# Attention 0 of a fused two-layer decoder: block 0 for all head groups first, then blocks 1 to 3 group by group, with the inputs of blocks 1 to 3 turned by DMA inside the first slots

## The reference, cut to what matters

```
q = (layernorm(x) @ wq).reshape(32, 64, 32, 128)
k = repeat((ctx @ wk).reshape(32, 64, 8, 128), 4)
v = repeat((ctx @ wv).reshape(32, 64, 8, 128), 4)
scores = einsum('bqhd,bkhd->bhqk', q / sqrt(128), k)
out = einsum('bhqk,bkhd->bqhd', softmax(scores), v)
x = x + out.reshape(32, 64, 4096) @ wo
x = x + ffn0(layernorm(x))        # fp8-like quantised weights W0, W1
x = x + attention1(layernorm(x), ctx)
x = x + ffn1(layernorm(x))
```

## Time and profile before

| | |
|---|---|
| median of 3 runs | 1656.03 us (1653.91 to 1657.03) |
| the profiled execution's own time | 1652.99 us |
| its span | 1651.3 us |
| PE busy, share of the span | 1499.1 us, 91% |
| DVE | 1237.5 us, 75% |
| ACT | 825.6 us, 50% |
| POOL | 267.0 us, 16% |
| first projection of attention 0 | at 56.95 us |
| scores of the first slot | at 74.68 us |
| last output product of attention 0 ends | at 1020.5 us |

### The profile page before, as it was taken

One profiled execution on the slowest core, in us unless ns is written; L12 is line 12 of the kernel. 1 busy time (PEld: TensorE's weight loads), 2 busy tenths in 40 slices (PEclk: granted clock), 3 DMA queues, 4 the chain that ended last, 5 costly groups with the idle time before them and its releaser, 6 DMA issues. The chain is left out here.

```text
span 1651.3 us, 29775 instructions
## 1 busy us (share of the span) xinstructions
PE 1499.1 (91%) x11322; PEld 796.1 (48%) x11323; DVE 1237.5 (75%) x2276; ACT 825.6 (50%) x1752; POOL 267.0 (16%) x247
## 2 busy tenths in 40 slices
PE   5799999999999999999999987799999988777695
PEld 4455455555555555555555553344444444344253
DVE  6567667668667667667767787799888885999777
ACT  3343433424324334243342332777888864888652
POOL 2001102002001011011011000001111103889620
PEclk7799999999999999999999998899999999999898
DMA  7032231321312313222221122122222350867502
GB/s 267 1 78 52 62 93 27 78 77 30 95 57 52 91 43 73 65 54 63 66 63 52 26 103 100 40 45 46 45 44 54 67 99 1 149 105 119 77 1 102
DMA packets 274121, 114.06 MB, mean 69 GB/s; under 512 B 239184, under 2 KB 255696, under 8 KB 273744
## 3 DMA queue, kind: packets, MB, share of 16 engines
q1 hardware_dynamic: 235104, 79.26, 22.2%
q10 hardware_dynamic: 38896, 33.03, 6.5%
HBM read 45.15 MB, written 11.53 MB: 34 GB/s over the span
## 5 line engine op out<-in xcount | busy, mean ns | idle before, releaser
L576 PE MATMUL pj<-XT,WQ 128*128 128x512 f16 x1536 | 338.9, 381 | 6.5 <-PEq L370 6.5
L618 PE MATMUL xp<-WO,OT 128*128 128x512 f16 x1536 | 340.5, 381 | 2.7 <-DVE X L815 2.7
L618 PEld LDWEIGHTS xp<-WO,OT 128*128 128x128 f16 x1536 | 148.3, 98 | 185.9 <-issue 14.9
L576 PEld LDWEIGHTS pj<-XT,WQ 128*128 128x128 f16 x1536 | 148.7, 98 | 182.1 <-DVE WKV L285 6.8
L696 ACT ACTIVATE E<-E 128x512 f32<-128x512 f32 x64 | 40.3, 629 | 328.1 <-DVE E L792 328.1
L815 DVE SCALAR_TENSOR_TENSOR X<-xp,X 128x512 f32<-128x512 f32 x128 | 88.4, 691 | 118.1 <-PE xp L618 117.1
L1019 PE MATMUL db<-W0T,XD 128*128 128x448 f16 x768 | 156.1, 362 | 16.5 <-DVE XD L1217 11.0
L556 POOL TENSOR_TENSOR VW<-VW,XB 128x1024 f32<-128x1024 f32 x14 | 33.0, 2357 | 770.4 <-DVE VW L98 770.4
L1037 PE MATMUL eb<-W1T,DT 128*128 128x512 f16 x672 | 147.7, 379 | 4.3 <-DMA DT<-HL 2.1
L757 DVE SCALAR_TENSOR_TENSOR QT<-pj,QT 128x512 f16<-128x512 f32 x128 | 88.1, 688 | 69.7 <-ACT QT L679 69.7
L1019 PEld LDWEIGHTS db<-W0T,XD 128*128 128x128 f16 x768 | 75.6, 100 | 94.8 <-DVE XD L1217 12.0
(11 more groups left out here) (228 smaller groups left out, 2388.7 us busy)
## 6 DMA issues: line engine op xcount, KB each, us to landing
W0T<-in_L_xattn_wq ACTq DMA_DIRECT2D x7, 1024.0 KB, 5.3
W0T<-in_L_xattn_wo ACTq DMA_DIRECT2D x7, 1024.0 KB, 5.1
CS<-in_ctx SPq DMA_DIRECT2D x4, 1024.0 KB, 10.0
X<-in_x SPq DMA_DIRECT2D x4, 1024.0 KB, 11.2
out<-X SPq DMA_DIRECT2D x8, 512.0 KB, 3.6
XB<-in_L_ffn_W ACTq DMA_DIRECT2D x28, 128.0 KB, 2.8
w0t<-XB ACTq DMA_DIRECT2D x7, 512.0 KB, 3.3
w1t<-W0T ACTq DMA_DIRECT2D x7, 512.0 KB, 3.8
```

The source lines that it names most:

```text
L576: last = pe.matmul(bank[:, :], w, src[:, b, k, tokens], start=n == 0, stop=n == 3 * KC - 1)
L618: last = pe.matmul(xp[i % 2][:, :], OT[:, a, j, i * P:(i + 1) * P], WO[:, b, j, :], start=n == 0, stop=n == 3 * REP - 1)
```

## The change

**Order.** Slots run in a new order: first block 0 of all 8 groups (`FIRST`, written out), then for each group its blocks 1 to 3 (`later`; groups 1 to 6 as a loop). The weights of each group are so loaded and split twice, 16 sets in place of 8. V has 3 buffers in place of 2.

**Start.** The separate start program is gone. Only block 0 is transposed by PE ahead of the first projection; x is loaded ahead of ctx. The projections of the first slot carry, on ACT and DVE, the split of the second group's WQ and WKV and the statistics of block 1.

**Inputs of blocks 1 to 3.** In each of the first six slots two x tiles and two ctx tiles are prepared: POOL normalises x, ACT writes the high parts (`high_inputs`, four copies of 128x512), POOL the low parts, and SP turns them by 8 DMA transposes of 128x512 f16 (`turn_inputs`) to XT and CT. DVE has the statistics of blocks 2 and 3 in slots 1 and 3.

**Moved pieces.** In the first slots ACT issues the load of WQ, WK, WV right behind the WO copy. In later slots WO's split is in t = 1, the first weight piece in t = 2 and 3, the second in t = 3 and t = 1 of the next group, the store in that t = 1. W0T is loaded at the end of the last group's t = 2.

The diff, cut to its core:

```diff
+        FIRST = [Slot(g, g, 0, g % 2) for g in range(GROUPS)]
+        def later(g, t):
+            return Slot(g * MORE + (GROUPS - 1 + t), g + GROUPS, t, t - 1)
 # SP
-            for g in range(GROUPS):
-                for t in range(SPG):
+            load_x(0)
+            sp.dma_start(C0, ctx[0:BLOCK, :].rearrange("(t p) d -> p t d", p=P)).then_inc(S["c_ld"], 16)
+            load_qkv(sp, 0)
+            sp.wait_ge(S["x_ld"], 16)
+            load_x(1)
+            sp.wait_ge(S["c_ld"], 16)
+            load_ctx(0)
+            sp.wait_ge(S["qkv_lo"], 2)
+            load_qkv(sp, 1)
+            load_o(sp, 0)
+            for b in (2, 3):
+                sp.wait_ge(S["x_ld"], 16 * b)
+                load_x(b)
+            def turn_inputs(s):
+                a, b = tiles_ahead(s)
+                for kind, (source, to) in enumerate(((XH, XT), (CH, CT))):
+                    sp.wait_ge(S["in_lo"], 2 * BT + 4 * s + 2 * kind + 2)
+                    for i in range(a, b):
+                        for part in range(2):
+                            sp.dma_start_transpose(to[:, part, :, i * P:(i + 1) * P], source[:, part, i - a, :]).then_inc(S["turned"], 16)
+                if s + 1 < AHEAD_SLOTS:
+                    load_ctx(s + 1)
+            for cur in FIRST:
+                turn_probabilities(cur)
+                if cur.n < AHEAD_SLOTS:
+                    turn_inputs(cur.n)
 # ACT
+            def first_slot(cur, nxt):
+                ahead = cur.n < AHEAD_SLOTS
+                probabilities(cur, nxt)
+                high_o(cur)
+                if cur.n < LAST:
+                    act.wait_ge(S["qkv_lo"], 2 * cur.n + 4)
+                    load_qkv(act, (cur.n + 2) % GROUPS)
+                high(nxt, (2,))
+                if ahead:
+                    high_inputs(cur.n, 0)
+                high(nxt, (3,))
+                if ahead:
+                    high_inputs(cur.n, 1)
+                high(nxt, (4,))
+                high_out(cur, 0)
+                high(nxt, (5,))
+                high_out(cur, 1)
+                if cur.n < LAST:
+                    high_q(act, cur.n + 2)
+                    high_kv(act, cur.n + 2)
+                act.wait_ge(S["o_lo"], cur.w + 1)
+                load_o(act, (cur.w + 1) % GROUPS)
+                if cur.n in (1, 3):
+                    ln_stats_scalar(act, 0, (2 + cur.n // 2,))
-            high(0, 0, range(6))
+            high_q(act, 0)
+            high_kv(act, 0)
+            high(FIRST[0], range(4))
+            high_q(act, 1)
+            ln_stats_scalar(act, 0, (1,))
+            high(FIRST[0], (4, 5))
+            high_kv(act, 1)
 # DVE
-                low(0, 0, u)
+            for u in range(4):
+                low(FIRST[0], u)
+            low_q(dve, 1)
+            dve.wait_ge(S["x_ld"], 32)
+            ln_moments(dve, 0, 1)
+            low(FIRST[0], 4)
+            ln_scales(dve, 0, 1)
+            low(FIRST[0], 5)
+            low_kv(dve, 1)
 # POOL
+            for s in range(AHEAD_SLOTS):
+                a, b = tiles_ahead(s)
+                pool.wait_ge(stats_ready, a // BT + 1)
+                if s:
+                    pool.wait_ge(S["in_lo"], 2 * BT + 4 * s - 2)
+                for i in range(a, b):
+                    normal(i)
+                for n, (full, split) in enumerate(((XN, XH), (XN, XH), (CS, CH), (CS, CH))):
+                    pool.wait_ge(S["in_hi"], 2 * BT + 4 * s + n + 1)
+                    pool.tensor_tensor(split[:, 1, n % 2, :], full[:, n % 2, :], split[:, 0, n % 2, :], ALU.subtract).then_inc(S["in_lo"], 1)
```

More of the change, by code:

```diff
@@ new lines, in _, with group @@
+            for cur in FIRST:
+                turn_probabilities(cur)
+                if cur.n < AHEAD_SLOTS:
+                    turn_inputs(cur.n)
+            def group(g, first, last):
+                for t in range(1, BLOCKS):
+                    turn_probabilities(later(g, t))
+                    if t == 1 and not first:
+                        turn_weights(g - 1, 1)
+                    if t == 3 and not last:
+                        turn_weights(g, 0)
+            group(0, True, False)
@@ L535, in load_weights @@
+            for g in range(1, LAST):
+                group(g, False, False)
+            group(LAST, False, True)
         def load_weights(queue, g):
@@ L641, in _, with slot, turned_before @@
-            pe.sem_inc(S["xp_done"], 1)
-            project(0, 0, range(6))
-            with pe.Fori(0, GROUPS - 1) as g:
-                group(g, False)
-            group(GROUPS - 1, True)
+            def slot(cur, nxt, turned=0):
+                scores(cur)
+                project(nxt, range(4), turned)
+                project(nxt, (4,))
+                weigh_values(cur, 0)
+                project(nxt, (5,))
+                weigh_values(cur, 1)
+            def turned_before(t):
+                return 16 * 8 * 2 * t
@@ new lines, in _ @@
+            pe.wait_ge(S["in_lo"], 2 * BT)
+            project(FIRST[0], range(6))
+            for cur in FIRST:
+                more = cur.n < LAST
+                slot(cur, FIRST[cur.n + 1] if more else later(0, 1), 0 if more else turned_before(1))
+                project_out(cur)
+            for t in range(1, BLOCKS):
+                cur = later(0, t)
+                slot(cur, later(0, t + 1) if t < MORE else later(1, 1), turned_before(t + 1) if t < MORE else 0)
+                project_out(cur)
@@ new lines, in _ @@
+            with pe.Fori(1, LAST) as g:
+                for t in range(1, BLOCKS):
+                    slot(later(g, t), later(g, t + 1) if t < MORE else later(g + 1, 1))
+                    project_out(later(g, t))
+            a, b, c = (later(LAST, t) for t in range(1, BLOCKS))
+            slot(a, b)
+            project_out(a)
+            slot(b, c)
+            scores(c)
+            project_out(b)
+            weigh_values(c, 0)
+            weigh_values(c, 1)
+            project_out(c)
@@ L907, in _, with probabilities @@
-            for u in range(6):
-                low(0, 0, u)
-            with dve.Fori(0, GROUPS - 1) as g:
-                group(g, False)
-            group(GROUPS - 1, True)
+            def probabilities(cur, nxt):
+                scores_less_max(cur, 0)
+                scores_less_max(cur, 1)
+                for jp in range(2):
+                    sums(cur, jp)
+                    low(nxt, jp)
+                    normalise(cur, jp)
+                low_probs(cur, 0)
+                low_probs(cur, 1)
+                low(nxt, 2)
```

626 lines of the change are left out of this document (318 added, 308 removed).

## The result

The changed kernel took 1686.37 us (median of 4 runs, 1685.48 to 1694.48), the kernel before 1654.97 us on the same chip (4 runs, 1651.53 to 1657.03). The ratio is 1.0205, 95% interval [1.0177, 1.0233]: slower by about 2%, where the forecast was 1644. The profiled execution has a span of 1683.7 us, 32.4 longer than the 1651.3 of before, at a mean granted clock of 0.963 (0.967 before).

A forecast was written before the change was run, and what follows sets the result against it. Attention 0 was taken to run at PE's own pace, its start bound by a POOL, PE, ACT, DVE chain. Terms -33.7 + 6.7 + 3.6 + 2.4 + 2.8 + 6.7 + 0.5 gave -11.0 us: forecast 1644, range 1632 to 1657.

The forecast's parts named there:

- part 5: Weight load beside PT in 7 first slots: 0.4 us of wait each, +2.8 us (0 to 25).
- rival C: PT's transposes get through only once the load's data is out: slower, 1666 to 1670; chance 0.09.
- part 3: Twice as many head group weight passes: a 0.51 us wait per added WO copy, 7 times, +3.6 us.
- Rival B: The load's and PT's queues share the engines evenly: PT lands 2.4 us later in 7 slots, 1649; chance 0.15.
- Part 1: The start: only block 0 is prepared ahead, so PE's first projection starts at 23.2 us, -33.7 us.
- Part 2: The seam to slot 0: scores wait 4.1 us for KT, then the next projection for WKV, +6.7 us (3 to 9).
- Part 4: Input splits in the first six slots cost nothing; LayerNorm statistics in slots 1 and 3 cost 1.2 each, +2.4 us.
- Part 6: Last group's t = 1 slot: extra DVE pieces make PE wait for QT and OT, +6.7 us (3 to 8).
- +0.5 for W0T: W0T's later load ends as the last PT transposes begin, and PE waits for these: +0.5 us (0 to 2).
- Rival D: The start doesn't shrink as told, or the seam costs double: 1652 to 1658, no change; chance 0.08.
- A: Small waits overlap or lie in slack, so parts 3, 4 and 5 are zero: about 1635; chance 0.20.

The follow-up runs named there:

- e4: The kernel before, with only the t = 0 slots' load of wq, wk, wv moved behind the WO copy, beside PT: 1707.04 us (1653.51 unmoved).
- e9: The changed kernel with wq loaded by four DMAs of 512-byte rows in place of one of 2 KB rows, still beside PT: 1680.34 us.
- e6: e1 with ACT's WO copy moved behind its third QT copy in the 16 slots that have one: 1632.67 us, ratio 0.9882.
- e1: The changed kernel with the load of wq, wk, wv issued at the head of each first slot, ahead of PT: 1648.5 us, ratio 0.9974.
- e3: The changed kernel with the weight load issued behind ACT's fourth QT copy, so behind PT's first issue: 1653.39 us, ratio 0.9996.

## Why the prediction was wrong

**The step that failed is part 5**, the price of the load beside PT. I had the bounds (0 and 3.6 us of wait per slot), took 0.4 "since PT is issued first", and put rival C at 0.09 on the ground that "packets of two queues have no reason to wait for a whole load". Both reasons fall. PT is not issued first: at 92.51 it is 0.2 us behind the load, and its second transpose follows at 93.80 with an issue of 4.13 us in place of 1.3. And PT was complete only when the load was out or nearly so, in the change, in e4 and in e9. The wait measured 3.3 to 4.6, above the upper bound in five of seven slots. (The prediction's own numbers, 5.1 us of load less 1.3 of slack, give 3.8 for that bound.) The loss of clock, which rival C had in words and the earlier trace rows in numbers, is another 1.9 per slot. So the term is +41.1 in place of +2.8: 38.3 of the 43.4 us by which the span missed the sum (1683.7 against 1640.3). Rival C named the mechanism; its 1666 to 1670 was still 16 us too low, by the size of the waits, by the clock, and by part 3. Rival B (even sharing, 1649) falls: it allows a landing of 5.2 us, and the seven slots have 7.8 to 9.0.

**Part 3 was mis-sized.** I priced each new WO copy at 0.51. Eight of the sixteen copies stand in t = 1 slots, and in seven of these, all but group 0's, PE waits 1.25. There DVE comes from a weight piece and starts the softmax 1.94 us behind the scores, not 0.90 as in a first slot, so its third query pass is 0.75 later (12.43 and 11.68 behind the scores):

```profile
430.82 2.76 PE L593 MATMUL pj<-CT,WKV 128*128 128x512 f16 x12 [1.25 <-DVE QT L860]
...
969.33 2.76 PE L593 MATMUL pj<-CT,WKV 128*128 128x512 f16 x12 [1.25 <-DVE QT L860]
```

Six such slots beside the last make 6 x 0.74 = +4.4 us. The mechanism was right: e6 removes it.

**Part 1** was right: -34.8 us at the first projection (-33.7 forecast). **Part 2** was right: the next projection is 28.7 us ahead of before, so the seam cost 34.8 - 28.7 = 6.1 (6.7), with a KT wait of 3.85 (4.1). **Part 4** was about right in size. For the statistics in slots 1 and 3 e1, free of PT waits, has extra QT waits of 1.1 and 1.5 us in slots 2 and 4 (1.2 each forecast). The input splits were not quite free: in e1 the V projection waits 0.26 us for QT in each of the six slots that have them, 1.6 us, and in none of the others (see POOL below). **Part 6** was right: the time from the scores of the last group's t = 1 slot to those that follow grew from 30.1 (932.90 to 962.99) to 35.8, by 5.7 us (6.7), with waits of

```profile
974.98 4.22 PE L598 MATMUL pj<-WKV,CT 128*128 128x128 f16 x48 [2.13 <-DVE QT L860]
980.82 0.83 PE L621 MATMUL tv<-PT,V 64*128 64x256 f16 x12 [1.61 <-DVE OT L869]
```

The +0.5 for W0T did not come as told: the PT wait there stayed (0.98, 0.99 before). But from the t = 2 slot's scores (991.95) to the end of attention 0 (1051.17) it is 59.2 us, before 57.5, with 4.3 us of waits for X in place of 2.8: +1.7.

The misses are then 38.3 + 4.4 - 1.1 - 0.6 - 1.0 + 1.2 = 41.2 of 43.4; 0.4 of the rest lies in the slots between. The stage behind attention 0, whose code is the same, took the other 1.8, 632.6 us in this profile and 630.7 in that of before. Over the twelve profiles of this document it took from 628.8 to 638.0 us, so 1.8 there is no finding, and a single run's time is to be read with that in mind.

Rival D (the start doesn't shrink) and A (small waits overlap) are both out by rows: the start shrank, and each small wait was paid.

**What stays open:** why SP's queue moves nothing at all beside the 2 KB rows and in bursts beside the short ones, and why the second issue is stretched. In particular, no run decides whether PT's packets stood ready and the engines served the other queue, or whether SP's queue got its work late. The first transpose's issue is as short as alone in slot 1 (1.24 us), and in slot 2 of e3 the second is late with an unstretched issue; so a long issue is not needed for the delay. The runs vary place, bytes and rows of the load, and give the delay for each; they don't look into the engines' turns.

## What to carry to other kernels

Look at what else is issued beside a transfer that an engine will wait for within a few microseconds. Here a 1.5 MB load issued at the same moment cost up to its whole time in each round, and PE paid again in clock behind the wait; 2.6 us ahead it still cost 0.3 to 2.7 us of wait, and behind PT's last issue nothing. When a term's bounds are 0 and 25 us and the sum's gain is 11, the term decides the sign; that no view shows the two together is a reason to give the upper bound real weight, not to choose near the lower. And an ordering of two copies on a helper engine, long ahead of short, is worth looking for wherever the list shows one small wait in every slot.

## What the runs showed of the hardware that I had not expected

- The issue of a transpose on SP can be stretched beside a load: slot 1's two take 2.58 us in e1, 3.46 with 512-byte rows, 4.86 with the load 2.6 us ahead, 5.42 in the change (up to 6.39). In slot 1 of the change it is the second that is long, 4.13 us; the first takes 1.24. Everything behind on SP is late by that too.
- DVE's pass over WO takes 3.26 us in place of 2.28 when POOL has just begun a subtraction, and POOL's next subtraction takes 3.19 us in place of 1.15 (timelines of slot 1, DVE and POOL; the last row is the second of POOL's four by itself):

```profile
95.37 6.53 POOL L563 TENSOR_TENSOR XB<-XB 128x512 f16<-128x512 f32 x4 [28.90 <-ACT XB L745]
95.41 3.26 DVE L873 SCALAR_TENSOR_TENSOR WO<-W0T,WO 128x2048 f16<-128x2048 f32 x1
96.49 3.19 POOL L563 TENSOR_TENSOR XB<-XB 128x512 f16<-128x512 f32 x1
```

  The other two of the four take 1.14 each, as the earlier trace rows has it. The times look as if each engine waited for the other: DVE's pass is 0.98 us longer, nearly the length of POOL's first subtraction, and POOL's second ends 1.0 us after DVE's pass. In e6 DVE's pass begins first (86.52, 2.29 us) and keeps its time, and POOL's first subtraction, begun 0.56 later, takes 2.74. In slots 6 and 7 of the change, without POOL's work, the pass takes 2.28. I had held POOL for an idle engine whose use is free. It cost nothing in the change, where PE waited for PT; in e1 it is the likely cause of the six waits of 0.26 us, since DVE's fourth query pass stands behind that pass.
- In the microseconds from 95 to 97, rows of 512 bytes beside PT brought the sum of both to 252 GB/s (e9), rows of 2 KB alone 379 (the change).
